# Six score banks instead of five in an attention and mixture-of-experts kernel: groups of four and two, the row-maximum jobs in a stretch of their own, an expert tile in three rounds

## The reference

```
xn = layernorm(x)
q, k, v = (xn @ W).heads * (cos(phase) * amplitude)
scores = (q k^T / sqrt(8)) * cos(2 pi (i - j) / S)
w = softmax(scores);  w = (w + roll(w, 1)) / sqrt(2)
attention = (w v) @ Wo
mixed = xn @ wqkv.T -> per token 8 expert logits, the best 2, softmax over the 2
experts = sum over the 2 of gate * (silu(a) * g) @ w2[e].T,   (a, g) = xn @ w1[e].T,  F = 352
out = x + attention + experts
```

## Time and profile before

| | |
|---|---|
| median of 3 runs | 587.59 us (587.22 to 587.95) |
| the profiled execution | 588.92 us |
| its span in the profile | 587.1 us, 19106 instructions |
| busy: PE, ACT, DVE, POOL | 93%, 89%, 38%, 16% of the span |

### The profile page before, as it was taken

One profiled execution on the slowest core, in us unless ns is written; L12 is line 12 of the kernel. 1 busy time (PEld: TensorE's weight loads), 2 busy tenths in 40 slices (PEclk: granted clock), 3 DMA queues, 4 the chain that ended last, 5 costly groups with the idle time before them and its releaser, 6 DMA issues.

```text
span 587.1 us, 19106 instructions
## 1 busy us (share of the span) xinstructions
PE 544.6 (93%) x7964; PEld 258.0 (44%) x7964; DVE 222.0 (38%) x521; ACT 521.4 (89%) x480; POOL 93.9 (16%) x102
## 2 busy tenths in 40 slices
PE   1978998889999999999999999999999999999875
PEld 1442333333454545445454544445445444454335
DVE  6876347602313424333333433243433131221312
ACT  2648988999999999999999999999999999999971
POOL 5200157543100101001010100100101010100000
PEclk9977999999999999999999999999999999999996
DMA  7852035434452332422333142413324222200402
GB/s 220 181 182 80 6 109 142 119 111 68 132 143 86 95 96 52 130 54 87 94 93 99 50 132 54 134 48 95 95 65 118 54 86 55 54 11 7 148 1 75
DMA packets 60890, 53.76 MB, mean 92 GB/s; under 512 B 33244, under 2 KB 50294, under 8 KB 60546
## 3 DMA queue, kind: packets, MB, share of 16 engines
q1 hardware_dynamic: 58082, 47.48, 30.2%
q0 software_dynamic: 2272, 4.72, 2.2%
q10 hardware_dynamic: 448, 0.30, 0.2%
HBM read 38.68 MB, written 13.78 MB: 89 GB/s over the span
## 4 chain that ended last, share of the span: by engine, by line
PE 69%; issue 12%; ACT 12%; DVE 3%; DMA 2%; SPq 1%; ACTq 0%; DVEq 0%
PE ps L1394 32%; PE ps L1370 21%; ACT big L702 12%; PE ps L1303 7%; PE ps L1313 4%; PE ps L1193 1%; PE ps L1340 1%; DMA acc<-in_L_attn_x 1%; DMA qk_parts<-store 1%; DVE store L785 1%; PE ps L1181 1%; PE ps L1204 0%; PE ps L1334 0%; DMA qa<-shift_rows 0%; PE ps L1226 0%
## 5 line engine op out<-in xcount | busy, mean ns | idle before, releaser
L702 ACT ACTIVATE big<-ps 128x1536 f32<-128x1536 f32 (+1 forms) x410 | 482.0, 1235 | 26.2 <-PE ps L1370 20.6
L1394 PE MATMUL ps<-big,vh 128*32 128x256 f32 (+1 forms) x3968 | 264.5, 392 | 0.0
L1370 PE MATMUL ps<-qa,ka 49*128 49x512 f16 x896 | 166.3, 388 | 17.3 <-ACT big L702 9.2
L1394 PEld LDWEIGHTS ps<-big,vh 128*32 128x32 f32 x3968 | 108.1, 109 | 110.6 <-issue 61.8
L1370 PEld LDWEIGHTS ps<-qa,ka 49*128 49x128 f16 x896 | 37.6, 94 | 137.7 <-ACT big L702 99.6
L598 POOL DMA_INDIRECT results<-y,row_of x39 | 38.0, 974 | 269.9 <-DVE y L997 268.5
L1303 PE MATMUL ps<-xgT,store 128*32 128x128 f32 x1716 | 65.2, 273 | 0.0
L1303 PEld LDWEIGHTS ps<-xgT,store 128*32 128x32 f32 x1716 | 54.1, 110 | 15.0 <-issue 2.3
L1060 DVE TENSOR_REDUCE m<-ps 128x1 f32<-128x512 f32 x64 | 44.1, 690 | 31.2 <-PE ps L1405 31.2
L982 DVE SCALAR_TENSOR_TENSOR cs<-cs,ps 128x384 f32<-128x384 f32 x39 | 21.6, 554 | 88.0 <-ACT cs L694 86.7
L997 DVE TENSOR_SCALAR y<-ps,weight_of 128x128 f32<-128x128 f32 x39 | 13.7, 351 | 98.8 <-PE ps L1313 98.8
(11 more groups left out here) (189 smaller groups left out, 220.3 us busy)
## 6 DMA issues: line engine op xcount, KB each, us to landing
store<-in_L_ffn_w SPq DMA_DIRECT2D x39, 352.0 KB, 3.2
store<-in_L_ffn_w SPq DMA_DIRECT2D x39, 192.0 KB, 3.3
qk_parts<-store SPq DMA_DIRECT2D x8, 512.0 KB
qa<-qk_parts SPq DMA_DIRECT2D x27, 128.0 KB
slots_x<-vh SPq DMA_DIRECT2D x8, 330.0 KB, 6.9
cs<-slots_x SPq DMA_DIRECT2D x80, 32.0 KB, 2.7
store<-results SPq DMA_DIRECT2D x4, 512.0 KB, 5.4
ka<-qk_parts SPq DMA_DIRECT2D x31, 64.0 KB
```

Of the source, the lines that this page charges most:

```text
L702: nc.scalar.activation(probs[:, prob_of(tiles[0]):prob_of(tiles[-1]) + 1, :], ps[:, bank_of(tiles[0]):bank_of(tiles[-1]) + 1, :], ACT.Exp, ...
L1370: ins = nc.tensor.matmul(ps[:, bank_of(n), :], k[at:at + KQ, P * o:P * o + P], q[at:at + KQ, CW * c:CW * c + CW], start=True, stop=True, t ...
L1394: ins = nc.tensor.matmul(ps[32 * c:32 * c + 32, O_BANKS[p % 2], cols], vh[:, p % 2, o + 8 * b, :], probs[:, prob_of(n), cols], start=k == ...
```

## The change

Bank 5 becomes a sixth score bank: groups of 4 and 2, RING = 6, 171 rounds, a store of 18 tiles, three half sets a round. The side bank is 6, and heads accumulate in bank 7 alone: a head's pieces end with a round, and its output is copied out in that round. The 64 jobs move from heads 4 to 11 into rounds 25 to 46, three a round, all in the side bank; the experts start at round 47, behind them, with three rounds a tile and a step in each. Only the exact heads' operands, now in a tile of their own, are loaded at round 21. `square_sums` and `turn_other` come at rounds 19 and 20.

More of the change, by code:

```diff
@@ L332, in quads_for, with job_at @@
             return (n - 1) // NC + 1
-        def job_in(half, k):
-            r, i = k // NT, k % NT
-            return r, i, half
+        def job_at(j):
+            return j // (2 * NT), j // 2 % NT, j % 2
         def near_keys(ap, i):
@@ L358, in rounds @@
         def rounds():
-            done, j, taken = 0, 0, [0, 0]
+            done = 0
             for r in range(ROUNDS + 1):
[L362 to L371, removed]
                 ready = min(RING * r, SCORE_TILES) // NC * HALVES
-                even = (RING * HALVES * r - NC) // NC - (2, 1, 1)[r - 2] if 2 <= r < 5 else (RING * HALVES * r - NC) // NC
-                pieces = range(done, max(ready if r == ROUNDS else min(ready, even), done))
+                head_ends = (done // (QUADS * HALVES) + 1) * QUADS * HALVES
+                even = RING * HALVES * r // NC - 1
+                pieces = range(done, max(min(ready if r == ROUNDS else min(ready, even), head_ends), done))
                 done = pieces.stop
-                yield r, jobs, pieces
+                yield r, jobs_of_round(r), pieces
+            assert done == H * QUADS * HALVES
         def quads_in(pieces):
@@ L527, in _ @@
                     sp.dma_start(carried[:], slots_x[0:TILES * P, DM:WITH_PLACE].rearrange("(n p) k -> p n k", p=P)).then_inc(carried_ld, 16)
[L528 to L534, removed]
                 if step == 1 and m + STAGES - 1 < TILES:
@@ L919, in choose @@
                 dve.wait_ge(mix_ps, 1)
-                then(nc.vector.tensor_copy(mix[:], ps[:, 5, 0:NT * 3 * E].rearrange("p (t n) -> p t n", t=NT)))
+                then(nc.vector.tensor_copy(mix[:], ps[:, SIDE_BANK, 0:NT * 3 * E].rearrange("p (t n) -> p t n", t=NT)))
                 then(nc.vector.tensor_tensor(pair[:], over_j(mix[:, :, 0:E]), over_e(mix[:, :, E:2 * E]), ALU.mult))
@@ L952, in assign_slots @@
                 dve.wait_ge(route_ld, 4 * 16)
-                then(nc.vector.tensor_scalar(tiles_of[:, 0, :], ps[:, 5, FP + E:FP + 2 * E], 1.0 / P, 0.5 - 0.5 / P, ALU.mult, ALU.add))
+                then(nc.vector.tensor_scalar(tiles_of[:, 0, :], ps[:, SIDE_BANK, FP + E:FP + 2 * E], 1.0 / P, 0.5 - 0.5 / P, ALU.mult, ALU.add))
                 then(nc.vector.tensor_scalar(tiles_of[:, 1, :], tiles_of[:, 0, :], ROUND, None, ALU.add))
@@ L957, in assign_slots @@
                 then(nc.vector.tensor_reduce(tiles_of[:, 3, :], before[:], AX, ALU.add))
-                then(nc.vector.scalar_tensor_tensor(tiles_of[:, 4, :], tiles_of[:, 3, :], float(P), ps[:, 5, FP:FP + E], ALU.mult, ALU.add))
+                then(nc.vector.scalar_tensor_tensor(tiles_of[:, 4, :], tiles_of[:, 3, :], float(P), ps[:, SIDE_BANK, FP:FP + E], ALU.mult, ALU.add))
                 then(nc.vector.tensor_tensor(slot_of, before_t[:, 0, 7:7 + NT, :], tiles_of[:, 4, :].unsqueeze(1).to_broadcast([P, NT, E]), ALU.add))
@@ L1248, in mix_tokens @@
             def mix_tokens(t):
-                ins = nc.tensor.matmul(ps[:, 5, 3 * E * t:3 * E * t + 3 * E], xnT[:, P * t:P * t + P], wqkvT[:], start=True, stop=True)
+                ins = nc.tensor.matmul(ps[:, SIDE_BANK, 3 * E * t:3 * E * t + 3 * E], xnT[:, P * t:P * t + P], wqkvT[:], start=True, stop=True)
                 if t == NT - 1:
@@ L1393, in weighted_values, with max_job, turn_maxima @@
                     _, o, c, b = tile_at(n)
[L1394 removed]
+                    ins = nc.tensor.matmul(ps[32 * c:32 * c + 32, O_BANK, cols], vh[:, p % 2, o + 8 * b, :],
                                            probs[:, prob_of(n), cols], start=k == 0, stop=u == QUADS * HALVES * (p + 1) - 1, tile_position=(0, 32 * c))
                 ins.then_inc(pv_done, HALVES if k == 0 else 1)
[L1398 removed]
+            def max_job(j):
+                h, i, c = job_at(j)
                 if j == 0:
                     pe.wait_ge(exact_ld, EXACT * 8 * 16)
[L1402 removed]
+                    pe.wait_ge(square_ready, 2)
+                    pe.wait_ge(shift_ready, 2)
                 after(pe, m_reduced, j)
                 at = 64 * c
[L1405 to L1406 removed]
+                nc.tensor.matmul(ps[:, SIDE_BANK, :], qe[at:at + KQ, h, P * i:P * i + P],
+                                 near_keys(ka[at:at + KQ, 2 + h, :], i), start=True, stop=True,
                                  tile_position=(at, 0)).then_inc(m_ready, 1)
[L1409 removed]
+            def turn_maxima():
                 pe.wait_ge(mx_ready, 1)
[L1411 to L1417 removed]
+                nc.tensor.transpose(ps[0:EXACT * NT, SIDE_BANK, 0:P], mx[:], ident[:]).then_inc(mxT_ready, 1)
             pe.wait_ge(wo_ready, 1)
@@ L1440, in _ @@
                     weighted_values(u)
-                    if u % HALVES == HALVES - 1:
-                        between(u // HALVES)
                 expert_work(r)
+                for j in jobs[2:]:
+                    max_job(j)
+                if r == JOBS_DONE - 1:
+                    turn_maxima()
             project_all(0)
```

63 lines of the change are left out of this document (25 added, 38 removed).

## The result

| | before | after |
|---|---|---|
| median (runs) | 587.77 us (587.22 to 588.14, 4) | 609.65 us (605.6 to 611.87, 4) |
| profiled execution, span | 588.92, 587.1 | 609.38, 607.6 |

The ratio is 1.0358 (95% interval 1.0328 to 1.0387): the change makes the kernel slower by 21.9 us, where the prediction had 606.3 in 596 to 616. The runs after the change spread over 6 us, those of before over 1. In what follows medians are over all executions, while ratios and intervals leave out two executions that the profile puts in the slower state (610.84 us in run 3, 658.8 us in run 5).

The account below looks back on a forecast made before the run. No single engine was taken to bound the kernel: PE and ACT pace each other in loops. Terms summed as times of day gave +18.7 us on 588.92, 607.6, so 606.3 us for the median, range 596 to 616.

Parts of the forecast that it names:

- Jobs in a chain: Rounds 25 to 45: each job waits for the previous maximum, 4.12 us a round where ACT needs 2.68; price 30.2 us.
- jobs cost nothing: Rival for the job rounds: jobs pipelined behind one another, the 30.2 us and waits around them vanish, 572 us; 5%.
- TensorE's clock falls in the job rounds: Rival: PE at 1.2 GHz in the job rounds, 57 us over 22 rounds, about 663 us; 3%.
- Norms: `square_sums` to `turn_other`, now one round between: 3.1 us lost against two plain rounds, 2.6 more than before.
- Exact operands: Loads of the exact heads' operands before job 0 in round 25: a wait of 0 to 5.5 us, 3 taken.
- Expert rounds: Three rounds an expert tile, a loop of PE and ACT: 9.16 us for 18 score tiles, 0.509 a tile after 0.514.
- Links 1 and 3: Expert loop: PE from group B to the next exponential, 3.04 us; exponential over B back to PE, 2.85 us.
- ACT with the tanh: Expert loop, ACT's own time in the round with the tanh: 1.78 + 0.98 + 0.51 = 3.27 us.
- The head ends: Pieces cut at head ends move a half set or two to the next round: 2 us over all expert rounds.
- The end: Adding of expert results ends near 588, about when the last copy is due; 1 us if this cover fails.
- The sum: Times of day added up to 589.3 against 570.58 us: +18.7 on an execution of 588.92, 606.3 for the median.

Follow-up runs that it names:

- run 3: The changed kernel with the three jobs of a round spread: after group A, after the first half set and after the second; 598.02 us, 1.0174.
- run 5: The changed kernel with groups of 3 and 2 put back, jobs, norms and three rounds an expert tile as changed; 648.36 us, 1.099.
- run 1: The changed kernel with each of the 64 maxima taken over every second column, softmax exponent scaled by 0.25; 591.29 us, 1.0072.
- run 2: The changed kernel without the 32 jobs over the second half of the keys and their maxima, exponent scaled by 0.25; 573.71 us, 0.977.
- run 8: The changed kernel, job rounds in groups of 3 and 2, jobs alternating two banks from round 27, norms one round later; 579.0 us; one-bank control 604.43 us.
- Run 4: The changed kernel with `turn_other`, shifts and head order one round later, jobs from round 27; 609.89 us; with results also added later, 606.0 us.
- run 6: The changed kernel without two of the three chunks of the product with w2 in every expert tile; 600.97 us, 1.022.

## Why the prediction was right, step by step

**Jobs in a chain.** Right, and the main term: 4.09 to 4.12 us a round against 4.12. That is a round without a fall of the clock; with the falls it was 4.41 on average (88.25 / 20). Runs 1, 2, 3 and 8 show the chain from four sides: a shorter maximum, fewer jobs, another order, another bank. The rival that jobs cost nothing fell; run 8 shows the condition that it lacked, a second bank.

**The clock.** The rival "TensorE's clock falls in the job rounds" was priced as a lasting fall of 57 us and given 3%. What happened lies between: it fell for 3.4 or 6.8 us at a time. From x(26) = 127.37 to x(46) = 215.62, 20 rounds, it was 88.25 us where 20 x 4.09 gives 81.8, so 6.4 us beyond the chain; the head ends of rounds 33 and 34 are part of that. That idle time on PE brings the falls about is supported but not shown. In the profiled executions of runs 1, 2 and 8 no fall lies in the job rounds after round 26, and PE's waits for a maximum sum to 7.8, 0.2 and 0.4 us, after 19.8 with the change. But in run 3 they sum to 6.8 us, less than in run 1, and the clock fell. Which idle time counts is open; of the falls, those at 160.8 after the change and at 159.1 in run 3 both follow round 33, which has one half set. The Trainium skill (TensorE: Matmul & The Clock Gate, A second HAM failure mode) describes such a fall from short idle times between groups; this trace agrees, with the waits of 0.35 and 0.57 us in a job round that the timeline shows. The spread of the runs after the change goes with the clock: 605.6, 609.4, 609.9 and 611.9 us at a mean granted clock of 0.973, 0.969, 0.967 and 0.959. The prediction also said of the low clock in the third and fourth slice of the kernel before that PE was hardly idle. PE was busy 17.08 of the 18.10 us before that fall, but in the low stretch itself, 38.1 to 51.8 us, only 8.59 of 13.70.

**Norms.** 5.1 us beyond two plain rounds (x(19) to x(21) was 4.89 + 5.57) against 3.1. The round of `turn_other`, which is what the prediction priced, cost 5.57 - 2.68 = 2.9 us: PE's wait was shorter than assumed (1.89 us instead of near 3; 105.47 - 100.85 = 4.6 us from squares to `turn_other`, not 5.6), but the half sets behind it ran at half clock (106.2 to 109.6). The other 2.2 us lie in round 19, where `square_sums` itself waited 1.57 us for DVE; the prediction had no such term, since before no wait stood there. Run 4 shows that the wait in round 20 is not simply added to the time: without it, the last copy waits for the adding of the results instead.

**Exact operands.** Job 0 was put at 120.7, it came at 122.00; the wait (1.04 us idle in the row) was smaller than the 3 us taken, because PE was late already.

**Expert rounds.** 9.16 us was forecast for a tile and 8.97 measured; (572.70 - 219.19) / 39 = 9.06 with the head ends. The loop was right, as runs 5 and 6 confirm, but the three rounds of a tile came as 3.07, 3.05 and 2.85 us where 3.2, 3.3 and 2.7 were written. Links 1 and 3 hold: the two rounds without the tanh sum to 3.07 + 2.85 = 5.92, against 3.04 + 2.85 = 5.89. The term "ACT with the tanh", 1.78 + 0.98 + 0.51 = 3.27, was mis-sized: it is 3.05. The 0.98 and the 0.51 were read off round 102 of the kernel before, in which PE's link ended at the same moment (307.20 + 0.64 = 307.84), so they held a wait for PE (the 0.98 too: `widen` ended at 306.43 + 0.84 = 307.27, the tanh began at 307.33). The head ends cost about 4.5 us instead of 2: a round with five half sets starts its step late, and the tanh waits for it.

**The end.** The adding of results ended at 592.74, "about when the last copy is due" (592.65). PE was done at 592.21, so the cover was just gone, at a cost of some 0.4 us.

**The sum.** The last copy was forecast at 589.3 and came at 592.65: x(47) 8 us late (early rounds 3, clock and head ends the rest), experts 5 us better. Two errors of opposite sign made the total look better than its parts: that the sum came within 3.4 us of 609.65 is partly luck. The mechanism of the main term was not. Rounds 12 and 24 start near 1 us late for a reason that I did not find.

## What to carry to other kernels

A small operation that another engine must read before its bank can be written again has a floor of its own: issue to reader, the reader's time, and back (here 0.42 + 0.69 + 0.06 = 1.17 us). Count how many of them a round holds, multiply by that floor and compare with the round; a second bank removes it, a faster order only lowers it. And when a time is read off the trace for one engine's loop, check that no other loop ends at the same moment there.

## What the runs showed of the hardware

PE's granted clock fell to half although the longest wait of PE between 125 and 161 us was 0.75 us and it was busy 76% of 131.5 to 156.4; before the fall at 160.8 us it was 2.89 of 4.40 us busy. With PE busy 31.5 of 32.6 us in the same stage of run 8 it stayed full. In run 3 it fell after 22.31 of 24.40 us busy and then 1.76 of 2.80.

A job in rows 64 to 127 of the array and the next group's first score, in rows 0 to 63, start together (147.38 both). Whether the job is free there depends on the count: three scores and a job took 0.60 us, as four scores do here without a job, but a job and four scores took 0.81 (143.29).
